# s_j of the graph layers brought to all partitions by two DMAs through DRAM in place of four TensorE transposes

## The reference, cut to what matters

```
si = x @ a[:256]                      # one number for each node i
sj = x @ a[256:]                      # one number for each node j
scores = si[:, None] + sj[None, :] + b          # 128 x 128
scores = where(scores >= 0, scores, 0.2 * scores)
scores = where(adj + eye > 0, scores, -inf)
attn = softmax(scores, axis=-1)
h = layernorm(x + attn @ x) * g1 + beta1
ff = gelu(h @ W1 + b1) @ W2 + b2                # 256 -> 1024 -> 256
x = layernorm(h + ff) * g2 + beta2
```

## Time and profile before

| what | value |
|---|---|
| median of 3 runs | 1720.91 us (1720.08 to 1721.85) |
| the profiled execution | 1720.4 us |
| its span, first to last instruction | 1718.6 us |
| mean granted TensorE clock | 0.98 |
| busy: TensorE, weight loads | 94%, 83% |
| busy: VectorE, ScalarE, GpSimd | 78%, 71%, 78% |
| DMA engines, all queues | about 23% of the span |
| the attention stage | to about 396 us |
| layers 0, 1, 2 | about 430 to 853, 853 to 1274, 1274 to 1718 us |

### The profile page before, as it was taken

The page is one execution under the profiler, slowest core; times in us unless marked ns, Lnnn a source line. Parts: engine busy times, 40 slices in busy tenths (PEclk is TensorE's granted clock), DMA queues, the critical chain, the costliest instruction groups (busy, mean ns, idle before and its releaser), DMA issues.

```text
span 1718.6 us, 40460 instructions
## 1 busy us (share of the span) xinstructions
PE 1607.4 (94%) x11904; PEld 1424.9 (83%) x11904; DVE 1347.8 (78%) x5298; ACT 1226.2 (71%) x2852; POOL 1335.0 (78%) x2389
## 2 busy tenths in 40 slices
PE   4999999983999999999899999999999999999994
PEld 3888888872899899899788998998988888888894
DVE  1889889896877877877878778778787887888862
ACT  1888888883677777777667777777776777777763
POOL 5688888863578778778687787787778999999996
PEclk8999999996999999999999999999999999999997
DMA  6132233332122112112122221121211223222211
GB/s 199 63 100 90 94 98 98 95 104 66 50 74 98 58 52 73 55 54 73 37 74 74 84 73 45 65 73 39 71 62 38 74 73 97 74 73 76 71 50 49
DMA packets 145980, 127.48 MB, mean 74 GB/s; under 512 B 16513, under 2 KB 136833, under 8 KB 145921
## 3 DMA queue, kind: packets, MB, share of 16 engines
q1 hardware_dynamic: 138880, 124.30, 22.6%
q10 hardware_dynamic: 7040, 2.51, 0.7%
HBM read 89.04 MB, written 37.75 MB: 74 GB/s over the span
## 4 chain that ended last, share of the span: by engine, by line
PE 52%; POOL 16%; DVE 5%; issue 2%; ACT 1%; POOLq 0%; DVEq 0%; ACTq 0%
PE ps L45 22%; PE ps L897 22%; PE ps L870 3%; POOL xo L810 2%; POOL gnn_n L160 2%; POOL gnn_norm L804 2%; PE ps L884 2%; POOL gnn_norm L160 2%; POOL gnn_fin L823 2%; DVE gnn_junk L1022 2%; POOL inv L155 2%; PE ps L862 1%; POOL gnn_hb L793 1%; POOL gnn_hb L789 1%; PE ps L877 1%
## 5 line engine op out<-in xcount | busy, mean ns | idle before, releaser
L897 PE MATMUL ps<-gnn_w_hi,gnn_g_hi 128*128 128x256 f32 x1536 | 434.2, 283 | 0.0
L897 PE MATMUL ps<-gnn_w_lo,gnn_g_hi 128*128 128x256 f32 x1536 | 429.0, 279 | 0.0
L897 PE MATMUL ps<-gnn_w_hi,gnn_g_lo 128*128 128x256 f32 x1536 | 428.7, 279 | 0.0
L992 ACT ACTIVATE gnn_g_hi<-ps,b_cols 128x512 fp32r<-128x512 f32 x384 | 264.6, 689 | 205.9 <-PE ps L45 205.7
L45 PE MATMUL ps<-gnn_hT_hi,gnn_w_hi 128*128 128x512 f32 x768 | 339.1, 442 | 4.1 <-DVE gnn_g_lo L1093 4.1
L1093 DVE TENSOR_TENSOR gnn_g_lo<-ps,gnn_g_hi 128x512 fp32r<-128x512 f32 x384 | 262.7, 684 | 96.0 <-ACT ps L993 95.5
L45 PE MATMUL ps<-gnn_hT_hi,gnn_w_lo 128*128 128x512 f32 x768 | 304.0, 396 | 0.0
L45 PE MATMUL ps<-gnn_hT_lo,gnn_w_hi 128*128 128x512 f32 x768 | 303.8, 396 | 0.0
L897 PEld LDWEIGHTS ps<-gnn_w_lo,gnn_g_hi 128*128 128x128 f32 x1536 | 288.9, 188 | 2.2
L897 PEld LDWEIGHTS ps<-gnn_w_hi,gnn_g_hi 128*128 128x128 f32 x1536 | 288.8, 188 | 2.2
L897 PEld LDWEIGHTS ps<-gnn_w_hi,gnn_g_lo 128*128 128x128 f32 x1536 | 288.7, 188 | 0.0
(11 more groups left out here) (127 smaller groups left out, 3967.4 us busy)
## 6 DMA issues: line engine op xcount, KB each, us to landing
hist<-xo SPq DMA_DIRECT2D x48, 512.0 KB, 3.8
x<-hist SPq DMA_DIRECT2D x48, 512.0 KB, 3.9
aw<-in_L_gnn_attn_w SPq DMA_DIRECT2D x48, 256.0 KB, 4.1
gmask<-mask_hist SPq DMA_DIRECT2D x48, 256.0 KB, 4.1
att_xT_raw<-in_xT SPq DMA_DIRECT2D x16, 512.0 KB, 3.4
att_xl<-in_x SPq DMA_DIRECT2D x16, 512.0 KB, 3.6
gnn_fin<-hist SPq DMA_DIRECT2D x16, 512.0 KB, 3.9
out<-gnn_fin SPq DMA_DIRECT2D x16, 512.0 KB, 3.0
```

Source lines behind the costliest of these rows:

```text
L897: mm = e.matmul(FF2[j % 2], g[a][:, m, j * N:(j + 1) * N], V[b][:, m, :], start=(n == 0), stop=(n == len(terms) - 1))
L992: e.activation(g[0][:, m, :], FF1[FFB[m]], ACT.Gelu, bias=bias)
```

## The change

`spread_sj` moves from TensorE to SyncE. It waits for aij_out, stores `s_j` to a row of DRAM (`sj_rows`, two of them, used in turn), element by element, since s_j lies across the partitions; waits for that store (sj_st); and loads the row of 4 x 128 numbers to all 128 partitions of the new SBUF tile `sj_b` (sj_ld). The transposes in TensorE's body and `first_spread` go. `masked_sums` waits for sj_ld and for exp_out of the step before, and reads `sj_b` in place of TB. `attention_sums` waits for the store of the step before in place of its transposes; `attention_shifts` gets a wait for pT_out. SyncE's program gets a spread for each step: 0, 1 and 2 ahead of the layers, and then that of t+3 behind the loads and the store in body t.

```diff
+    sj_rows = nc.dram_tensor("sj_rows", [2, GROUP, N], F32).ap()
...
+            sj_b = sb("sj_b", [P, GROUP, N])
...
+            sj_st, sj_ld = sems("sj_st", "sj_ld")
...
+                def spread_sj(t2, par2):
+
+                    e.wait_ge(aij_out, t2 + 1)
+                    with nc.allow_non_contiguous_dma(reason="a column for each graph, 2 KB in all"):
+                        e.dma_start(sj_rows[par2].rearrange("j p -> p j"), s_j[:]).then_inc(sj_st, 16)
+                    e.wait_ge(sj_st, 16 * (t2 + 1))
+                    if not isinstance(t2, int) or t2:
+                        e.wait_ge(u_out, t2)
+                    e.dma_start(sj_b[:].rearrange("p j n -> p (j n)"),
+                                sj_rows[par2:par2 + 1].rearrange("o j n -> o (j n)").to_broadcast([P, GROUP * N])
+                                ).then_inc(sj_ld, 16)
...
                 e.wait_ge(ln_out, START + NG)
                 e.dma_start(block_of(hist, NG - 1), xo[1][:]).then_inc(stored[1], 16)
+                spread_sj(0, 0)
                 for t in range(2):
                     e.dma_start(fin[t][:], block_of(hist, t)).then_inc(fin_ld[t], 16)
                 e.wait_ge(y1_out, GROUP)
                 load_step(e, 2, 0, 1)
+                spread_sj(1, 1)
+                spread_sj(2, 0)
                 pairs = NG // 2
 
                 def pair_of_steps(q):
                     load_ahead(q, 1)
                     store_x(q, 0)
+                    spread_sj(2 * q + 4, 0)
                     load_ahead(q + 1, 0)
                     store_x(q, 1)
+                    spread_sj(2 * q + 5, 1)
 
                 load_ahead(0, 0)
+                spread_sj(3, 1)
                 with e.Fori(0, L - 1) as l:
                     pair_of_steps(l * pairs)
                     e.wait_ge(w1_split, 2 * (l + 1))
@@ -752,11 +773,14 @@
                         pair_of_steps(l * pairs + p)
                 first = (L - 1) * pairs
                 load_ahead(first, 1)
+                spread_sj(2 * first + 4, 0)
                 with e.Fori(first + 1, L * pairs - 2) as q:
                     for par in range(2):
                         load_ahead(q, par)
                         store_out(q - 1, par)
+                        spread_sj(2 * q + par + 3, 1 - par)
                 load_ahead(L * pairs - 2, 0)
+                spread_sj(T - 1, 1)
                 for t in range(T - 6, T):
                     store_out(t // 2, t % 2)
...
-                def spread_sj(t2):
-
-                    e.wait_ge(aij_out, t2 + 1)
-                    e.wait_ge(pT_out, t2 - 1)
-                    for j in range(GROUP):
-                        mm = e.transpose(TB[:, j * N:(j + 1) * N], s_j[:, j:j + 1].to_broadcast([P, N]), ident[:])
-                    mm.then_inc(sjT_made, 1)
...
@@ -914,26 +930,15 @@
                         if more >= 1:
                             for j in {0: (0, 1), 3: (2,), 4: (3,)}.get(m, ()):
                                 aggregate(t1, p1, j)
-                        if more >= 2 and m == 5:
-                            spread_sj(t + 2)
                     e.wait_ge(w2_split, 2 * (layer_of(t) + 1))
                     for j in range(GROUP):
                         ffn2(t, j, more)
 
-                def first_spread(t2):
-
-                    e.wait_ge(aij_out, t2 + 1)
-                    for j in range(GROUP):
-                        mm = e.transpose(TB[:, j * N:(j + 1) * N], s_j[:, j:j + 1].to_broadcast([P, N]), ident[:])
-                    mm.then_inc(sjT_made, 1)
-
                 e.wait_ge(x_ones, 2)
-                first_spread(0)
                 probs_T(0)
                 for j in range(GROUP):
                     aggregate(0, 0, j)
                 e.wait_ge(pT_out, 1)
-                first_spread(1)
                 e.wait_ge(p_out, 2)
...
@@ -1017,7 +1022,7 @@
                     if j == 0:
                         e.wait_ge(g_ld[par2], 32 * (half2 + 1))
                         if not isinstance(t2, int) or t2:
-                            e.wait_ge(sjT_made, t2)
+                            e.wait_ge(sj_st, 16 * t2)
...
                 def masked_sums(t2, par2, half2):
                     e.wait_ge(m_ld[par2], 32 * (half2 + 1))
-                    hold_dve(e, sjT_made, t2 + 1)
-                    for j in range(GROUP):
-                        ins = e.tensor_tensor_reduce(out=u[:, j, :], in0=TB[:, j * N:(j + 1) * N], in1=mask[par2][:, j, :],
+                    if not isinstance(t2, int) or t2:
+                        e.wait_ge(exp_out, t2)
+                    hold_dve(e, sj_ld, 16 * (t2 + 1))
+                    for j in range(GROUP):
+                        ins = e.tensor_tensor_reduce(out=u[:, j, :], in0=sj_b[:, j, :], in1=mask[par2][:, j, :],
                                                      scale=1.0, scalar=LOWEST, op0=ALU.add, op1=ALU.max,
                                                      accum_out=top[:, j:j + 1])
...
+                    if not isinstance(t2, int) or t2:
+                        e.wait_ge(pT_out, t2)
                     e.tensor_scalar(shift, s_i[:], ab[par2][:, 0:1], None, ALU.add).then_inc(bias_step, 1)
```

More of the change, by code:

```diff
@@ L647, in gnn_kernel @@
             out_stored = sems("out_stored_even", "out_stored_odd")
+            sj_st, sj_ld = sems("sj_st", "sj_ld")
             fin_sum, bn3_out, mv3_out, ln3, norm3_out, fin_out = sems(
                 "fin_sum", "bn3_out", "mv3_out", "ln3", "norm3_out", "fin_out")
-            (w1_hi_set, w1_split, w2_hi_set, w2_split, x_ones, ff1_made, gelu_out, g_lo_out, pT_made, pT_out, agg_made, aij_out, sjT_made,
+            (w1_hi_set, w1_split, w2_hi_set, w2_split, x_ones, ff1_made, gelu_out, g_lo_out, pT_made, pT_out, agg_made, aij_out,
              u_out, bias_step, bias_out, exp_out, p_out, recip_out, y1_out, bn1_out, mv1_out, ln1, n1_out, hb_out,
@@ L654, in gnn_kernel @@
                     "w1_hi_set", "w1_split", "w2_hi_set", "w2_split", "x_ones", "ff1_made", "gelu_out", "g_lo_out", "pT_made", "pT_out",
-                    "agg_made", "aij_out", "sjT_made", "u_out", "bias_step", "bias_out", "exp_out", "p_out",
+                    "agg_made", "aij_out", "u_out", "bias_step", "bias_out", "exp_out", "p_out",
                     "recip_out", "y1_out", "bn1_out", "mv1_out", "ln1", "n1_out", "hb_out", "hT_made", "hT_hi_out",
```

## The result

The changed kernel takes 1843.49 us (median of 4 runs, 1839.07 to 1848.95), against 1721.24 us for the kernel before on the same chip: ratio 1.0714, 95% interval 1.0699 to 1.0728. It is 7.1% slower; forecast were 1745 us and at most 1765. The profiled execution has a span of 1838.2 us, 119.6 us more than before, at a mean granted TensorE clock of 0.96.

The account below looks back on a forecast made before the run. TensorE was taken to set about half the chain of waits, GpSimd a sixth. Entry +12.2, layers 0 and 1 0, layer 2 and the turn +12.6 gave +24.8 us: 1745 us, 1.4% slower, range 1721 to 1765.

Parts of the forecast that it names:

- Cost 0: In the steps, the two added DMAs were to cost nothing; without cover, 7 us a step.
- rival 3: In the steps, the two DMAs do not fit in 12.15 us; at 2 us too late 1835 us; chance 0.04.
- a store that lands later than 6 us: Sign, named in advance, that the forecast is wrong: the store of s_j landing later than 6 us.
- The store of s_j: SyncE's store in 512 pieces of 4 bytes each step, taken as 3.0 us; bounds 2.3 and 5.4 us.
- The load of sj_b: SyncE's load of 256 KB each step, taken as 3.0 us, between 2.3 and 4.8 us.
- The cover of 12.15 us: In the steps, time from the last attention sum (664.59) to the masked sums that need it (676.74), to hide both DMAs.
- The entry: Ahead of the layers nothing covers the DMAs: +7.6 us for spread 0, +4.6 for spread 1, together +12.2 (9 to 20).
- Layers 0 and 1, without the DMAs: 0: Layers 0 and 1: VectorE's masked sums stand about 0.3 us against 0.28 us idle, so gain 0 (-8.1 to +4 us).
- the bound of 29 x 0.28 = 8.1 us: Layers 0 and 1: most that 29 steps could gain, VectorE moving up only by its 0.28 us idle time.
- rival 1: The port does not matter, masked sums stay at 0.29 us: +4.1, 1724.5 us (1719 to 1730); chance 0.13.
- rival 4: VectorE stands for every GpSimd instruction and loses each time: +50, 1770 us (1757 to 1775); chance 0.15.
- Layer 2, +0.9 us a step: Layer 2: masked sums meet GpSimd's instructions, making g_lo late; 0.9 us a step over 13 steps, +11.7 us.

Follow-up runs that it names:

- apart_256: Changed kernel with the load reading x_in and the store's 512 pieces of 4 bytes written 256 bytes apart in DRAM; 1737.79 us, ratio 1.0100.
- load_only: Changed kernel without the store of s_j and the wait for it, its 256 KB load reading x_in instead; 1735.46 us, ratio 1.0081.
- before_no_tr: Kernel before the change without the four transposes in TensorE's body, masked sums still reading PSUM; 1709.90 us, ratio 0.9936.

## Why the prediction was wrong

Its direction was right, its size was not. The step that failed is "Cost 0": two DMAs of 3.0 + 3.0 us and a us for issue and waits, under 12.15 us of cover. What happened is rival 3, held for 0.04: at 2 us too late a step it had 1835 us. The prediction also named the sign: a store that lands later than 6 us.

- **The store of s_j**, 3.0 us with bounds of 2.3 and 5.4. Measured 8.24 us a wait in the changed kernel. The bounds came from small loads of scattered numbers; they were the nearest rows, with 256 and 1024 pieces of 4 bytes, but they were reads from DRAM, and this is a write. The direction alone does not explain the miss: apart_256 shows that 512 pieces of 4 bytes, written apart, take 2.1 us, just under the bounds; written side by side they took four times that. What the working left out is where the pieces of a write fall.
- **The load of sj_b**, 3.0 us with bounds of 2.3 and 4.8. Measured 3.2 by itself, close to the prediction, but 5.5 in the changed kernel, over the bound. Some 1.5 us of the growth are a late start of the load, 0.9 us the loads issued behind it; why it starts late stays open.
- **The cover of 12.15 us.** Right for layers 0 and 1: load_only, with masked sums at their old place, shows 12.1 us again. In the step shown the chain is 8.1 + 5.5 = 13.6 us, on average 14.1, since it is often longer (the s_j ready at 683.28 is used at 697.86, 14.6 us later). That is 2.0 us too late, and the step grows by 1.9: the rival's price, "each us a us", holds. In layer 2 the cover was only 11.0 us (in the kernel before the last s_j of a step is there at 1354.73 and used at 1365.76), which the prediction did not look at; the 11.2 us of its upper bounds would not have fitted there. The chain of 14.0 us is 3.0 us too late, and the step grows by 1.9.
- **The entry**, +12.2 us (9 to 20). Measured +29.6. The store of spread 0 was issued at 402.25 (predicted 402.75), but SyncE issued the load at 411.14, and the masked sums came at 417.79, 15.9 us later than before, with two loads of fin right behind sj_b. In spread 1 the store took 9.9 us and the load 3.2: 12.0 us more. The last 1.7 us come until the masked sums of step 2. With the load alone (load_only) the entry costs 11.9, with the quick store of apart_256 15.8. So even with a quick store the middle of 12.2 was low, though inside its bounds.
- **Layers 0 and 1, without the DMAs: 0.** Right. The first masked sum stands: 0.59 against 0.28, 0.31 us for predicted 0.25 to 0.4. The step is 25.87 us against 25.90. The gain without the port is 0.37 us a step (before_no_tr), so the bound of 29 x 0.28 = 8.1 us was 2.7 us short. Rivals 1 and 4 fall: rival 1 would have had 25.6, rival 4 more than 25.9 in every second step.
- **Layer 2, +0.9 us a step.** Mis-sized. The masked sums last 2.4 us there (1593.57 to 1595.94 in load_only) against 0.92, 1.45 us longer, so that part came as predicted, but the step grows by 0.15 us (322.99 against 321.21 over twelve). The working set 1.4 to 2.2 us against TensorE's 0.76 us before L884 and left out the 0.44 us that its own transposes no longer take: there were 1.2 us to spare, and before_no_tr shows them (12.2 us before L884 in ten steps). In load_only TensorE stands 0.84 us a step for g_lo and no longer for n1. before_no_tr, with no SBUF input, has the same 26.9 us, so this growth does not need the port; why a step without the transposes is 0.15 us longer is not shown.

In the prediction's terms the measured sum is 29.6 (entry) + 53.9 (29 steps of layers 0 and 1, where it had 0) + 22.7 (twelve steps of layer 2, where it had 0.9 each for the port) + 13.4 (turns and end) = 119.6 us.

The part of the Trainium skill that was weighed (SBUF — State Buffer, "Who interferes with whom") agrees with load_only's 0.59 against 0.28 us. On the failed step the Trainium skill (DMA: Bandwidth & Descriptors, "Specifications") says that transfers under 512 bytes are done by read-modify-write. By the traces a size under 512 bytes alone does not make the wait long, since 4-byte pieces apart and 16-byte pieces side by side are both quick. The same page of the Trainium skill ("Anatomy of one DMA", for DMAs that GpSimd issues; these are SyncE's) says that the semaphore waits for the receipt of the last write, some 2 us in all. apart_256 agrees (2.1 us), and in the changed kernel the wait of 6.6 us without a packet looks like a long such receipt. That neighbouring 4-byte writes read and rewrite the same stretch of DRAM one after another would explain both; it was not shown.

## What to carry to other kernels

A small transfer on a chain is priced by how long until its semaphore comes, and here that hung on where the pieces of a write fall: as they lie in SBUF (16 bytes) or 256 bytes apart they were quick, as 4-byte neighbours they were not. With 16-byte pieces the reading engine takes the stride, which cost 0.3 us a step here. A bound for an operation that no row shows has to come from a row of the same direction and the same placement; where there is none, the upper end is open, and a step with a cover of 12 us is not free. The cover itself is to be read in each stage: it was 12.1 us in layers 0 and 1 and 11.0 in layer 2. And work taken off the bounding engine pays only when the engine that feeds it has room at that place: with VectorE's input in SBUF it paid only once VectorE's order had been changed as well, with its input in PSUM (before_no_tr) it paid at once.

## What was not expected of the hardware

- 512 pieces of 4 bytes written side by side into 2 KB of DRAM: a wait of 8.2 us on average and 10.2 at most. In the step looked at, all packets were recorded in the first 1.5 us, and nothing moved in the 6.6 us until the wait ended. The same pieces 256 bytes apart: 2.1 us to landing. 128 pieces of 16 bytes, side by side: the load behind them was issued 1.4 us after the store in the median, 3.8 at most.
- Behind such a store a load of 256 KB often starts late: its first packet comes 2.5 us after the issue (median), 1.0 in the kernels without that store. Store and load trade: in the 16 steps in which the load was issued more than 9 us after the store it took 4.2 us, in the others 5.8. From the last s_j to the masked sums it is 13.3 to 15.6 us in the steps.
- An entry that is 26 us shorter can make the whole slower (1863 against 1843 us): at 29.3 us a step TensorE's granted clock was 0.97, at 28.0 it was 0.99. Which of the two brings the other is not shown.
